# Summing 48 units of a pairwise bilinear stage along the free axis

## What is computed

```python
e = stack([tbl_f[ids[:, f]] for f in range(40)], axis=1)      # 512 x 40 x 64
viW = einsum('bpd,pde->bpe', e[:, i_idx, :], L0_rec_W)         # 780 pairs i < j, one 64 x 64 matrix each
z = einsum('bpe,bpe->bp', viW, e[:, j_idx, :])                 # 512 x 780
h = concatenate([z, dense_ctx], axis=1)                        # 512 x 796
h = maximum(h @ W_top1 + b_top1, 0.0)                          # 512
h = maximum(h @ W_top2 + b_top2, 0.0)                          # 256
y = h @ W_top3                                                 # 1
```

## Time and profile before

| | |
|---|---|
| median of three runs | 365.91 us |
| the profiled execution | 367.68 us |
| its span, first to last instruction | 365.9 us |
| granted TensorE clock, mean | 0.995 |
| TensorE busy | 349.1 us (95%) |
| VectorE busy | 259.1 us (71%) |
| ScalarE busy | 38.4 us (10%) |
| GpSimd busy | 153.9 us (42%) |

### The profile page before, as it was taken

The page is one execution under the profiler, slowest core; times in us unless marked ns, Lnnn a source line. Parts: engine busy times, 40 slices in busy tenths (PEclk is TensorE's granted clock), DMA queues, the critical chain, the costliest instruction groups (busy, mean ns, idle before and its releaser), DMA issues.

```text
span 365.9 us, 4723 instructions
## 1 busy us (share of the span) xinstructions
PE 349.1 (95%) x1848; PEld 118.1 (32%) x1848; DVE 259.1 (71%) x271; ACT 38.4 (10%) x61; POOL 153.9 (42%) x261
## 2 busy tenths in 40 slices
PE   0989979999999999999999999999999999999997
PEld 0332223333323333333333333333333333333342
DVE  3956688378787787665768787887668687877430
ACT  1010300030100301010000300000000001200232
POOL 2888888337776754443534453253223000000000
PEclk9999989999999999999999999999999999999999
DMA  6961122002722222112202221122022000000000
GB/s 205 409 246 22 23 79 75 20 14 73 277 83 64 92 77 72 59 22 73 68 11 73 72 69 23 58 71 68 13 65 68 5 0 2 0 0 3 0 1 0
DMA packets 11448, 24.29 MB, mean 66 GB/s; under 512 B 3857, under 2 KB 3857, under 8 KB 11298
## 3 DMA queue, kind: packets, MB, share of 16 engines
q1 hardware_dynamic: 7330, 19.79, 15.4%
q0 software_dynamic: 4096, 4.20, 5.5%
HBM read 23.98 MB, written 0.00 MB: 66 GB/s over the span
## 4 chain that ended last, share of the span: by engine, by line
PE 87%; issue 8%; DVE 2%; DMA 1%; ACT 1%; SPq 0%; DVEq 0%
PE y_ps L477 45%; PE z_ps L500 24%; PE t_ps L456 4%; PE y_ps L508 3%; PE t_ps L447 2%; PE t_ps L429 2%; PE y_ps L429 2%; PE y_ps L538 2%; DVE one_hot L385 1%; DMA x<-in_ids_one_hot 1%; PE y_ps L483 1%; DVE prod L407 1%; ACT x L321 1%; PE t_ps L544 0%; ACT prod L363 0%
## 5 line engine op out<-in xcount | busy, mean ns | idle before, releaser
L407 DVE TENSOR_TENSOR prod<-y_ps,x 128x1024 f32<-128x1024 f32 x190 | 221.0, 1217 | 75.7 <-PE y_ps L477 74.4
L477 PE MATMUL y_ps<-x,w_sb 64*128 64x512 f32 x760 | 182.5, 610 | 4.9 <-ACT x L321 2.3
L308 POOL DMA_INDIRECT rows<-in_tbl,ids_sb x128 | 122.7, 958 | 129.6 <-PE y_ps L477 92.7
L477 PEld LDWEIGHTS y_ps<-x,w_sb 64*128 64x128 f32 x760 | 67.0, 186 | 109.3 <-issue 58.2
L500 PE MATMUL z_ps<-prod,selector 128*32 128x512 f32 x780 | 95.3, 604 | 0.0
L500 PEld LDWEIGHTS z_ps<-prod,selector 128*32 128x32 f32 x780 | 20.6, 110 | 67.9 <-issue 37.7
L429 PE MATMUL t_ps<-one_hot,table 128*64 128x512 f32 x96 | 22.8, 631 | 8.4 <-DVE one_hot L385 8.4
L385 DVE TENSOR_SCALAR one_hot<-x,numbers 128x512 f32<-128x512 int32 x64 | 27.2, 496 | 4.9 <-DMA x<-in_ids_one_hot 4.9
L303 POOL MEMSET spacer<- 128x128 f32 x127 | 30.5, 240 | 0.1
L321 ACT ACTIVATE x<-t_ps 128x512 f32<-128x512 f32 x18 | 10.8, 597 | 188.8 <-PE t_ps L447 149.9
L456 PE MATMUL t_ps<-z_sb,w_sb 128*128 128x512 f32 x32 | 15.9, 618 | 0.0
(11 more groups left out here) (30 smaller groups left out, 36.1 us busy)
## 6 DMA issues: line engine op xcount, KB each, us to landing
w_sb<-in_w_units SPq DMA_DIRECT2D x25, 512.0 KB
x<-in_ids_one_hot SPq DMA_DIRECT2D x8, 256.0 KB, 4.9
table<-in_small_tables SPq DMA_DIRECT2D x8, 256.0 KB, 4.8
rows<-in_tbl,ids_sb POOLq DMA_INDIRECT x128
w_sb<-in_w SPq DMA_DIRECT2D x1, 1792.0 KB
w_sb<-in_w SPq DMA_DIRECT2D x1, 512.0 KB
ids_sb<-in_ids SPq DMA_DIRECT2D x1, 80.0 KB, 4.7
z_sb<-in_dense_t SPq DMA_DIRECT2D x1, 32.0 KB
```

Source lines behind the costliest of these rows:

```text
L308: pool.indirect_dma_start(rows[:, n % ROW_SLOTS, bt, h * D:(h + 1) * D], None, tables[f], bass.IndirectOffsetOnAxis(ap=ids_sb[:, bt, f:f + ...
L407: dve.tensor_tensor(prod[:, at:at + 2, :], y_ps[:, s % Y_SLOTS], leaf, ALU.mult).then_inc(prod_ready, 1)
L477: ins = pe.matmul(y_ps[:, slot, h, :], w_sb[own, c % W_SLOTS, at:at + P], x[own, m, :], start=True, stop=True)
```

## The change

From pair 8 on, the cross units with m = 1, 3, 5 and 7 are taken out (four for each of twelve k), and 48 rows units ("rows", k, bt) come in their place, four for each k, one per 128 examples. The steps stay 195. A rows unit turns the product round: 64 x 128 of `x[k]` (one tile of the batch) are the weights, and 64 x 512 of `w_rows_sb` stream, so that the batch lies on the partitions and the eight matrices of one field of pair k against the eight fields of pairs 1, 3, 5, 7 lie in the free axis. VectorE multiplies the 128 x 1024 result by the gathered rows themselves, kept untransposed in `kept`, into one of four slots of `row_prod`. The 16 sums of 64 elements are then taken along the free axis: for two units of three by ScalarE in 16 instructions with `accum_out`, for every third by VectorE in one `reduce_sum`. They land in `z_rows`, are transposed by two jobs "z_turn" and fill two of the late banks. Rounds are counted over the 147 other units alone: 37.

Rows units stand one after each 2.2 other units (steps 31 to 185). `LEAD` goes from 3 to 5, mix from 4 to 6 steps ahead, partial pieces stand 4 steps apart instead of 6, weight slots go from 6 to 4, gather slots from 6 to 4 beside the four kept, pacing begins at pair 12; the tile `table` shares memory with tiles that are written later. Weights of the rows units come in twelve groups of 256 KB, two slots, in SyncE's queue between the chunks.

```diff
+KEPT = (1, 3, 5, 7)
+ROWS_FROM = 8
+ROW_PROD_SLOTS = 4
+ROW_W_SLOTS = 2
+ROW_DVE = 3
+ROW_EVERY = 2.2
-W_SLOTS = 6
+W_SLOTS = 4
-ROW_SLOTS = 6
+ROW_SLOTS = 4
+ROW_LAG = 2
-LEAD = 3
+LEAD = 5
-PARTIAL_EVERY = 6
+PARTIAL_EVERY = 4
-PACED_FROM = 9
+PACED_FROM = 12
...
+        own = [("cross", m, k) for m in range(k) if k < ROWS_FROM or m not in KEPT]
...
+    start = units.index(("cross", 0, ROWS_FROM))
+    behind = [[] for _ in units]
+    for i in range(BT * (NP - ROWS_FROM)):
+        k, bt = ROWS_FROM + i // BT, i % BT
+        behind[max(start + int(ROW_EVERY * i), units.index(("cross", 0, k)) + 2 * bt)].append(("rows", k, bt))
+    units = [u for unit, more in zip(units, behind) for u in [unit] + more]
...
-        jobs_at[max(FIRST[4 * q + 3], s - 4)].append(("mix", q))
+        jobs_at[max(FIRST[4 * q + 3], s - 6)].append(("mix", q))
...
+    jobs_at[ROWED[BT * GROUPS_IN_BANK - 1] + 8].append(("z_turn", 0))
+    jobs_at[STEPS - 2].append(("z_turn", 1))
...
+def rows_by_dve(n):
+    return n % ROW_DVE == ROW_DVE - 1
...
+            def load_row_weights(j):
+                if j >= ROW_W_SLOTS:
+
+                    sp.wait_ge(y_ready, ROWED[BT * (j - ROW_W_SLOTS + 1) - 1] + 1)
+                else:
+                    sp.wait_ge(turned, TURN_SEQ["look", LOOKS[-1]] + 1)
+                sp.dma_start(w_rows_sb[:, j % ROW_W_SLOTS, :],
+                             w_rows[j]).then_inc(w_rows_loaded[j % ROW_W_SLOTS], 16)
...
+            def sum_rows(s):            # ScalarE
+                _, k, bt = UNITS[s]
+                act.wait_ge(prod_ready, s + 1)
+                for h in range(2):
+                    for n in range(2 * len(KEPT)):
+                        own = row_prod[:, NUMBER[s] % ROW_PROD_SLOTS, h, D * n:D * n + D]
+                        column = row_sum(k, h, n)
+                        ins = act.activation(own, own, ACT.Copy, accum_out=z_rows[:, bt, column:column + 1])
+                ins.then_inc(rows_on_act, 1)
...
+                if s >= ROW_LAG and UNITS[s - ROW_LAG][0] == "rows" and not rows_by_dve(NUMBER[s - ROW_LAG]):
+                    sum_rows(s - ROW_LAG)
...
+            def sum_rows(s):            # VectorE
+                _, k, bt = UNITS[s]
+                first = row_sum(k, 0, 0)
+                dve.wait_ge(prod_ready, s + 1)
+                dve.reduce_sum(z_rows[:, bt, first:first + ROW_SUMS],
+                               row_prod[:, NUMBER[s] % ROW_PROD_SLOTS].rearrange("p h (n e) -> p (h n) e", e=D),
+                               axis=mybir.AxisListType.X).then_inc(rows_on_dve, 1)
...
+                if unit[0] == "rows":   # VectorE, multiply
+                    if n >= ROW_PROD_SLOTS:
+
+                        wait_rows_summed(dve, n - ROW_PROD_SLOTS)
...
+                    leaf = kept[:, unit[2]:unit[2] + 1, :, :].rearrange("p o n d -> p o (n d)").to_broadcast([P, 2, B])
+                    dve.wait_ge(y_ready, s + 1)
+                    dve.tensor_tensor(row_prod[:, n % ROW_PROD_SLOTS], y_ps[:, s % Y_SLOTS], leaf,
+                                      ALU.mult).then_inc(prod_ready, 1)
+                    return
...
+                if UNITS[s - 1][0] == "rows" and rows_by_dve(NUMBER[s - 1]):
+                    sum_rows(s - 1)
...
+                if unit[0] == "rows":   # TensorE, multiply
+                    _, k, bt = unit
+                    for h, own in enumerate((low, high)):
+                        ins = pe.matmul(y_ps[:, slot, h, :], x[own, k, P * bt:P * bt + P],
+                                        w_rows_sb[own, (k - ROWS_FROM) % ROW_W_SLOTS, :], start=True, stop=True)
+                    ins.then_inc(y_ready, 1)
+                    return
```

More of the change, by code:

```diff
@@ L64, in plan_units @@
 def plan_units():
-    units, first = [], {}
+    units = []
     for k in range(1, NP):
-        first[k] = len(units)
-        cross = [("cross", m, k) for m in range(k)]
+        own = [("cross", m, k) for m in range(k) if k < ROWS_FROM or m not in KEPT]
         if k % 4 == 3:
-            cross.insert(min(k, 6), ("inner", k // 4))
-        units += cross
-    return units, first
+            own.insert(min(k, 6), ("inner", k // 4))
+        units += own
+    start = units.index(("cross", 0, ROWS_FROM))
[4 more added lines that the diff above has]
+    units = [u for unit, more in zip(units, behind) for u in [unit] + more]
+    return units, {k: units.index(("cross", 0, k)) for k in range(1, NP)}
 UNITS, FIRST = plan_units()
 STEPS = len(UNITS)
[L79 to L85, removed]
+SUMMED = [s for s, u in enumerate(UNITS) if u[0] != "rows"]
+ROWED = [s for s, u in enumerate(UNITS) if u[0] == "rows"]
+NUMBER = {s: n for units in (SUMMED, ROWED) for n, s in enumerate(units)}
+CHUNKS = -(-len(SUMMED) // CHUNK)
+ROUNDS = -(-len(SUMMED) // ROUND)
+EARLY_BANKS = 2 * PARTIAL_PAIRS
+ROW_BANKS = (EARLY_BANKS, EARLY_BANKS + 1)
+BANKS = EARLY_BANKS + 3
+ROW_GROUPS = NP - ROWS_FROM
+GROUPS_IN_BANK = P // ROW_SUMS
+REST_ROWS = ROW_SUMS * (ROW_GROUPS - GROUPS_IN_BANK)
+DENSE_ROW = REST_ROWS
+assert STEPS == 195 and EARLY_BANKS * BANK_ROUNDS < ROUNDS <= (EARLY_BANKS + 1) * BANK_ROUNDS
+assert len(ROWED) == BT * ROW_GROUPS and REST_ROWS + N_DENSE <= P
 INNER_AT = {u[1]: s for s, u in enumerate(UNITS) if u[0] == "inner"}
@@ L127 @@
 JOBS = [job for at in JOBS_AT for job in at]
-TURNS = [job for job in JOBS if job[0] in ("look", "turn", "partial")]
+TURNS = [job for job in JOBS if job[0] != "mix"]
 TURN_SEQ = {job: n for n, job in enumerate(TURNS)}
@@ L134, with plan_row_groups, last_of_round, dlrm_tower @@
 LOOKS = [job[1] for job in TURNS if job[0] == "look"]
+def plan_row_groups():
+    at = []
+    for j in range(ROW_GROUPS):
+        free = ROWED[BT * (j - ROW_W_SLOTS + 1) - 1] if j >= ROW_W_SLOTS else FIRST[EARLY_PAIRS - 1]
+        at.append(max(c for c in range(CHUNKS) if c < W_SLOTS or SUMMED[CHUNK * (c - W_SLOTS + 1) - 1] <= free))
+    return at
+ROW_GROUP_AT = plan_row_groups()
 assert LOOKS == list(ONE_HOT_PAIRS)
 def round_at(s):
-    r, rest = divmod(s - SUM_LAG - (ROUND - 1), ROUND)
-    return r if rest == 0 and r >= 0 else None
-def dlrm_tower(nc, ids, ids_one_hot, row_numbers, small_tables, tables, dense_t, w_units, w1, b1, w2, b2, w3, out):
+    last = s - SUM_LAG
+    if last >= 0 and UNITS[last][0] != "rows" and NUMBER[last] % ROUND == ROUND - 1:
+        return NUMBER[last] // ROUND
+    return None
+def rows_by_dve(n):
+    return n % ROW_DVE == ROW_DVE - 1
+def last_of_round(r):
+    return SUMMED[min(ROUND * r + ROUND, len(SUMMED)) - 1]
+def dlrm_tower(nc, ids, ids_one_hot, row_numbers, small_tables, tables, dense_t, w_units, w_rows, w1, b1, w2, b2, w3, out):
     ctx = ExitStack()
@@ L230, in dlrm_tower, with rows_of, rows_ap, wait_rows_summed @@
         out_stored = sem("out_stored")
+        def rows_of(n):
+            if n < len(KEPT):
+                return n, 1
+            return len(KEPT) + (n - len(KEPT)) % ROW_SLOTS, (n - len(KEPT)) // ROW_SLOTS + 1
+        def rows_ap(n, bt):
+            place, _ = rows_of(n)
+            return kept[:, bt, place, :] if n < len(KEPT) else rows[:, place - len(KEPT), bt, :]
+        def wait_rows_summed(eng, n):
+            eng.wait_ge(rows_on_act, sum(not rows_by_dve(i) for i in range(n + 1)))
+            if n >= ROW_DVE - 1:
+                eng.wait_ge(rows_on_dve, sum(rows_by_dve(i) for i in range(n + 1)))
         def wait_turn_done(eng, n):
@@ L554, in lay_out_units @@
     laid = np.zeros((CHUNKS, P, CHUNK, P), w.dtype)
-    for s in range(STEPS):
+    for s in SUMMED:
+        c, at = divmod(NUMBER[s], CHUNK)
         for rows, bank, half, i, j in pairs_of(s):
@@ L558, in lay_out_units, with lay_out_rows @@
             m = w[number[(i, j)]] if i < j else w[number[(j, i)]].T
-            laid[s // CHUNK, D * rows:D * rows + D, s % CHUNK, w_columns(s, bank, half)] = m
+            laid[c, D * rows:D * rows + D, at, w_columns(s, bank, half)] = m
     return laid.reshape(CHUNKS, P, CHUNK * P)
+def lay_out_rows(w):
+    number = pair_numbers()
+    laid = np.zeros((ROW_GROUPS, P, B), w.dtype)
+    for k in range(ROWS_FROM, NP):
+        for h, n, i, j in row_pairs(k):
+            i, j = ORDER[i], ORDER[j]
+            laid[k - ROWS_FROM, D * h:D * h + D, D * n:D * n + D] = (
+                w[number[(i, j)]] if i < j else w[number[(j, i)]].T)
+    return laid
 def lay_out_top1(w):
@@ L570, in lay_out_top1 @@
             laid[row, z_bank] = w[number[(min(i, j), max(i, j))]]
-    laid[DENSE_ROW:DENSE_ROW + N_DENSE, BANKS - 1] = w[len(number):]
+    for k in range(ROWS_FROM, NP):
+        for h, n, i, j in row_pairs(k):
+            z_bank, row = divmod(row_sum(k, h, n), P)
+            i, j = ORDER[i], ORDER[j]
+            laid[row, ROW_BANKS[z_bank]] = w[number[(min(i, j), max(i, j))]]
+    laid[DENSE_ROW:DENSE_ROW + N_DENSE, ROW_BANKS[1]] = w[len(number):]
     return laid
```

120 lines of the change are left out of this document (78 added, 42 removed).

## The result

The changed kernel takes 357.57 us (median of four runs, 357.39 to 357.76), the kernel before 366.05 beside it: ratio 0.9764, interval 0.9743 to 0.9784, 8.5 us faster. Its span is 356.0 us; 355.7 was forecast for the span. All four executions of the changed kernel had a mean granted clock of 0.995, as the profiled one of the kernel before. Span against span, at that same clock, the gain is 9.9 us.

A forecast was written before the change was run, and what follows sets the result against it. TensorE alone was taken to bound the middle stretch. The sum was 91.7 + (250.7 - 21.0 + 10.7) + 23.6 = 355.7 us of span, range 345 to 365.

The forecast's parts named there:

- TensorE's saving of 21.0 us: Middle stretch: 12 rounds of sums fewer save 22.2 us, two added turns cost 1.2; net 21.0 us less.
- The fourth rival: Rows units cost TensorE more than 0.907 us; 0.1 us each would make 5 us, 360 in all; no own chance.
- VectorE's reduction, taken at 1.15 us: 16 VectorE reductions of 128x1024 to 16 numbers at 1.15 us each, adding 18.4 us to VectorE.
- The loss of 10.7 us: Among rows units, level TensorE and VectorE with three product slots lose 0.087 us a step over 123 steps.
- second rival: ScalarE's late copies make TensorE wait at a pair's first unit, up to 4 us; 361 us in all; chance 0.12.
- the 0.907 us a unit: TensorE's matmuls in the middle: 0.907 us for each cross unit, taken unchanged for a rows unit.
- VectorE starves 0.65 us at a round: At a round VectorE has 2.45 us of multiplies left, but the next unit takes 3.1 us to reach it.
- "level" stretches: Steps 31 to 83: TensorE 67.8 us, VectorE 67.7; steps 99 to 168: TensorE 88.1, VectorE 89.3.
- ScalarE's sum, taken at 330 ns: ScalarE's 512 small sums in rows units, 330 ns each, 5.3 us a unit; ScalarE would just keep up.
- the third rival: ScalarE's sums become the bound; slower than before from 0.424 us a sum, 405 us at 0.50; chance 0.13.
- that hides it, barely: Turns five steps ahead (6.9 us) hide ScalarE's turn copies behind one unit's sums (5.3 us) and the copy (0.6).
- Gathers in time without pacing: GpSimd's pairs 9, 10, 11 unpaced arrive at 80, 91, 103 us, turns at about 91, 101, 111; no wait.

The follow-up runs named there:

- the pieces apart: Changed kernel with the first partial pair's pieces 3 steps later (the last one 5); 353.22 us when repeated, 360.71 us in a first, disturbed measurement.
- The half rounds: First partial pair's pieces later, second pair's one step later, each round of sums cut in two halves, the second two steps behind, against the changed kernel; 354.68 us.
- the doubled sums: Changed kernel with each of ScalarE's 512 sums done twice, the extra one into a scratch tile; 416.52 us, ratio 1.1365.
- the old pacing: Changed kernel with GpSimd's pacing from pair 9 on, not from pair 12; 360.99 us against 357.91 us unedited.
- the first group: Four kernels: changed kernel with shortened VectorE reductions 361.01 us, ScalarE sums twice 416.52, first pair's pieces later 360.71; kernel before with only the change's settings 370.88.
- the undisturbed repeats: Later runs without pauses: changed kernel with first partial pair's pieces later, 353.22 us; with VectorE's reductions reading 4 of each 64 elements, 352.97 us.

## Why the prediction was right

The total came out at 356.0 against 355.7 us of span, and so did each stretch: 92.0 (91.7 forecast), 240.5 (240.4), 23.5 (23.6). The mechanism, product slots between two level engines, is shown; that the middle agrees to 0.1 us is partly luck, as the third point tells. Point by point:

- TensorE's saving of 21.0 us: twelve rounds at 1.85 are gone (588 records), a rows unit costs TensorE what a cross unit does (0.86 and 1.06 us in the chain, line 618). The fourth rival is out.
- VectorE's reduction, taken at 1.15 us: 1209 ns each, the next start 1.13 later. Right.
- The loss of 10.7 us: 240.5 - 229.7 = 10.8. The size was right; its make-up was only partly so. 2.5 us were not VectorE's but ScalarE's copy ahead of the first partial piece (2.4 came back with the pieces apart). That is the second rival's mechanism at a place it did not name: not a pair's first unit, but a job in the same step as a turn, sharing its bank. The waits for slots are 9.4 us. The two make 11.9, not 10.8, so TensorE's own work was about 1.1 us under the forecast's 229.7. The step that was mis-sized there is likely the 0.907 us a unit: it is a mean over units beside a round (0.96) and between units (0.86), and with twelve rounds fewer more of them are of the second kind. Two errors met with opposite signs.
- "VectorE starves 0.65 us at a round, unless a reduction lies just then in its queue": the rows agree, 0.85 us behind rounds where none lies there (idle before the multiply at 124.38), none where one does (the reduction at 155.49). I counted the reductions as full VectorE work among the "level" stretches, and the experiments show that they mostly fill the gaps: without 15 of their 19 us only 3.7 us come back. The other 5.4 us of slot waits stay; 5.8 multiplies at 1.13 to 1.16 us stand there between two rounds, against three slots. The half rounds remove them. No run had another number of slots, so that three are too few is read from these waits and not tried.
- ScalarE's sum, taken at 330 ns: 240. The fixed part and the hand-out overlap, which no row of before could show. By the formula of the Trainium skill (ScalarE: Activation LUTs, What ACT_TABLE_LOAD costs), 186 ns + 0.833 ns per element, the instruction at 64 elements is an estimated 239 ns, and the trace has 242: it agrees. The error cost nothing in the total, since ScalarE did not bind at either. It kept the third rival at 0.13 that deserved less; the doubled sums confirmed its mechanism, with 416.5 us at 0.48 us a sum. That ScalarE would be 90% busy among the rows units was wrong with it: it was 60% busy in the middle (143.3 of 240.5 us).
- TensorE's busy time, "about 328 us", was 333.9, because a unit that starts late is counted as busy.
- The copies: "that hides it, barely" was right for the pairs and wrong for the piece.
- Gathers in time without pacing: right, and with the old pacing they are not, by 3.2 us. I had costed this edit at nothing; it is rather a condition of the gain, since the shorter rhythm brings the turns forward.
- The median: 357.57, 1.9 over the forecast, because I carried the span. The profiled execution of before had a span of 365.9, but most later runs of that kernel with a mean granted clock of 1.0 instead of 0.995 have spans near 364. All four runs of after had 0.995. The median being equal to the span was chance; adding the 1.8 us that lie around the span would have given 357.5.

## What to carry to other kernels

When two engines are level by sum, look for the longest block of work that one of them does without feeding the other, and measure it against the slots between them: here it was a round of 1.85 us against three slots. Work added to the starving engine then costs little (15 us for 3.7 here), and splitting the block costs a restart at every cut. A busy engine can be waiting: late starts showed only when start was set against start. When an idle engine is given long runs of small instructions, look at every job that waits for one of its copies, not only at its total: one piece in a turn's own step cost 2.5 us with the engine 45% busy. Compare stretches between two fixed events when medians differ by 1 or 2 us, and look at the granted clock inside them first.

## What was not expected

A summing ScalarE instruction over 64 elements is two in the trace (242 and 188 ns) at 240 ns for both. TensorE's granted clock fell in the kernel with doubled sums: full speed is 2.4 GHz, its other level 1.2, and the mean from 110 to 360 us was 0.91, with five single waits of 5.3 to 10.7 us in which TensorE did nothing; eight records of unit matmuls took 3.70 us behind a wait of 5.29, where 1.99 is usual. How much of the 18 us over the expected time the clock makes is not shown. The pauses of the first group, 2 to 6 us between 85 and 103 us on all engines but GpSimd, came in all four kernels there, in none of the eight later ones, and by its times not in the kernel before on the same chip (365.92 to 367.58 in 11 runs). Their cause stays open; what they share, gathers without a pause up to 103 us, was there in the undisturbed repeats as well.
